# Reordering a written-out schedule: attention values one chunk earlier, turned norm tiles inside the feed-forward layer, ranking gathered before attention

## The reference

```
x = x + 0.5 * ffn(layernorm(x))
x = x + attn(layernorm(x))
x = x + 0.5 * ffn(layernorm(x))

ffn(x):   scores = x @ w_router; the 768 best of 1024 tokens: x <- gelu(x @ w_block); others keep x
attn(x):  Q = x @ Wq.T (16 heads of 32);  latent_k = x @ Wk_down.T;  latent_v = x @ Wv_down.T (64 wide)
          logits = (Q_h @ q_to_latent_h) @ latent_k.T / 8, causal; attn = softmax
          heads = (attn @ latent_v) @ v_up_h;  out = heads @ Wout.T
```

## Time and profile before

| | |
|---|---|
| median of 3 runs | 2322.88 us (2321.43 to 2325.64) |
| the profiled execution | 2322.91 us |
| its span | 2320.8 us |
| PE busy | 2143.9 us (92%) |
| DVE busy | 1762.1 us (76%) |
| ACT busy | 1099.7 us (47%) |
| POOL busy | 490.1 us (21%) |
| DMA, mean over 16 engines | 53 GB/s, 15% of their time |

### The profile page before, as it was taken

The page is one execution under the profiler, slowest core; times in us unless marked ns, Lnnn a source line. Parts: engine busy times, 40 slices in busy tenths (PEclk is TensorE's granted clock), DMA queues, the critical chain, the costliest instruction groups (busy, mean ns, idle before and its releaser), DMA issues.

```text
span 2320.8 us, 52537 instructions
## 1 busy us (share of the span) xinstructions
PE 2143.9 (92%) x21256; PEld 1305.3 (56%) x21256; DVE 1762.1 (76%) x5017; ACT 1099.7 (47%) x1942; POOL 490.1 (21%) x574
## 2 busy tenths in 40 slices
PE   5689999999999999999999999999999999999997
PEld 4444477545774456744566446764466544765446
DVE  6668857887678876798778886788857888578747
ACT  3335643556425554255543565445643456435562
POOL 3101212123112231023210232112221113121132
PEclk8789999999999999999999999999999999999999
DMA  4301021210312103021021211212021120212000
GB/s 140 145 1 37 4 73 48 99 39 2 99 48 74 38 18 94 38 74 39 20 91 38 75 39 36 74 56 67 29 69 41 66 83 2 73 37 74 2 2 37
DMA packets 71934, 123.16 MB, mean 53 GB/s; under 512 B 2832, under 2 KB 33040, under 8 KB 67600
## 3 DMA queue, kind: packets, MB, share of 16 engines
q1 hardware_dynamic: 71696, 119.81, 15.0%
HBM read 81.53 MB, written 37.75 MB: 51 GB/s over the span
## 4 chain that ended last, share of the span: by engine, by line
PE 77%; DVE 12%; ACT 5%; issue 4%; POOL 1%; DMA 1%; DVEq 0%; POOLq 0%; SPq 0%; ACTq 0%
PE psum L871 27%; PE psum L884 18%; PE psum L1011 11%; PE psum L1018 10%; PE psum L887 5%; DVE part L1160 3%; ACT pr L851 3%; PE psum L898 2%; DVE psum L1162 2%; PE psum L923 2%; DVE junk L1110 1%; DVE junk L1112 1%; PE psum L965 1%; DVE junk L1095 1%; DVE qk L1149 1%
## 5 line engine op out<-in xcount | busy, mean ns | idle before, releaser
L851 ACT ACTIVATE pr<-psum 128x512 f32<-128x512 f32 x1152 | 617.7, 597 | 528.9 <-PE psum L887 528.8
L884 PE MATMUL psum<-qk,qk 32*128 32x512 f32 (+3 forms) x4608 | 516.1, 370 | 62.6 <-DVE part L1160 26.7
L1162 DVE CUSTOM_DVE_ANT_0 psum<-psum,mask_b 128x512 f32<-128x512 f32 (+3 forms) x1024 | 473.1, 522 | 106.0 <-PE psum L898 104.0
L884 PEld LDWEIGHTS psum<-qk,qk 32*128 32x128 f32 x4608 | 318.6, 186 | 385.7 <-ACT pr L851 339.0
L898 PE MATMUL psum<-qk,qk 32*128 32x512 f32 (+3 forms) x4608 | 511.8, 370 | 21.5 <-DVE part L1160 18.8
L1160 DVE TENSOR_REDUCE part<-psum 128x1 f32<-128x512 f32 x512 | 325.1, 681 | 56.0 <-PE psum L898 53.7
L898 PEld LDWEIGHTS psum<-qk,qk 32*128 32x128 f32 x4608 | 311.2, 186 | 43.9 <-DVE part L1160 23.0
L1011 PE MATMUL psum<-pr,v_sb 128*32 128x512 f32 (+3 forms) x3072 | 314.1, 504 | 1.6 <-ACT ht L753 1.6
L1018 PE MATMUL psum<-pr,ones 128*32 128x512 f32 (+3 forms) x3072 | 306.8, 494 | 0.0
L745 POOL TENSOR_SCALAR_AFFINE_SELECT pr<-pr 128x512 f32<-128x512 f32 x256 | 161.6, 650 | 563.0 <-ACT pr L851 561.0
L871 PE MATMUL psum<-wb_h,nt_h 128*128 128x512 f32 x512 | 207.6, 405 | 16.2 <-DVE wb_l L1059 12.3
(11 more groups left out here) (116 smaller groups left out, 3372.8 us busy)
## 6 DMA issues: line engine op xcount, KB each, us to landing
nt_raw<-x_turned_dram SPq DMA_DIRECT2D x16, 1024.0 KB, 6.8
x<-x_dram SPq DMA_DIRECT2D x16, 1024.0 KB, 7.1
spill_x<-x SPq DMA_DIRECT2D x16, 1024.0 KB, 4.7
x<-spill_x SPq DMA_DIRECT2D x16, 1024.0 KB, 6.6
out_dram<-x SPq DMA_DIRECT2D x14, 1024.0 KB, 5.1
w_h<-scratch_o SPq DMA_DIRECT2D x28, 256.0 KB, 3.1
w_l<-scratch_o SPq DMA_DIRECT2D x28, 256.0 KB, 3.3
w_h<-scratch_q SPq DMA_DIRECT2D x6, 1024.0 KB, 4.9
```

Of the source, the lines that this page charges most:

```text
L851: nc.scalar.activation(pr_of(b, g, u)[:, 2 * p + place, :], bank(e, place), ACT.Exp, scale=SCALE).then_inc(exp_ready, 1)
L884: eng.matmul(o, (k_h, k_h, k_l)[t][own, P * j:P * (j + 1)], (q_h, q_l, q_h)[t][own, queries], start=(t == 0 and at == 0), stop=False, skip ...
L1162: m = nc.vector.tensor_tensor_reduce(scores, scores, mask_b[:, BANK - w:BANK], 1.0, FAR, ALU.add, ALU.max, top_of)
```

## The change

The values move from chunk 2n (unit n-2) to chunk 2n+1 (unit n-1), the denominators from chunk 2n+1 to chunk 2n; so the order PV(n-2), DEN(n-2) becomes DEN(n-2), PV(n-1), also at the end of group 3, where PV of unit 7 now stands in chunk 17. In `project` the first two turned tiles of the second norm go ahead of the last F. K and V of tiles 2 to 7 each stand a place or two earlier. In `back` NM goes behind the dots, both SC behind F of tile 2, and four of the eight RT stand before the attention instead of two. In `opening` the layer's F start after the ranking's events. Ring G gives way to an order of banks taken from `queue` at F of tile 2.

```diff
@@ opening
-        out += [("WC", 0), ("WS", 0)] + sum([raw(0, i) for i in range(TC, NT)], [])
+        out += [("WC", 0)] + sum([raw(0, i) for i in range(TC, NT)], [])
...
-        out += layer(0, 0, 0) + layer(0, 0, 1) + [("SC", 0, 0, 0), ("SC", 0, 0, 1), ("WS", 1), ("WS", 2)]
-        out += [("RT", 0, 0, i) for i in range(NT)]
-        for i in range(2, NT):
+        out += [("SC", 0, 0, 0), ("SC", 0, 0, 1), ("WS", 0)] + [("RT", 0, 0, i) for i in range(NT)] + [("WS", 1), ("WS", 2)]
+        for i in range(NT):
@@ project
-        out += layer(0, b, 6) + summed(b, 5) + [("NO", 1, b, 1)] + layer(0, b, 7)
-        after = [summed(b, 6), [], [], summed(b, 7) + scales(1, b, 1)]
-        for i in range(TC):
-            out += [("T", 1, b, i)] + ([("NO", 1, b, i + 2)] if i + 2 < TC else []) + left[i] + after[i]
+        out += [("NO", 1, b, 1)] + layer(0, b, 6) + [("T", 1, b, 0), ("NO", 1, b, 2), ("T", 1, b, 1), ("NO", 1, b, 3)]
+        out += summed(b, 5) + layer(0, b, 7) + left[0] + [("T", 1, b, 2)] + summed(b, 6) + left[1] + [("T", 1, b, 3)]
+        out += left[2] + left[3] + summed(b, 7) + scales(1, b, 1)
...
-        out += [("Q", b, 0, 1)] + loads[0] + keys[1] + [("V", b, 1)] + splits[0] + splits[1]
-        out += [("Q", b, 1, 1)] + loads[1] + maxima(b, 0, 0) + splits[2] + [("Q", b, 2, 1)] + loads[2] + maxima(b, 0, 1) + splits[3]
-        out += keys[2] + [("V", b, 2), ("Q", b, 3, 1)] + loads[3] + maxima(b, 0, 2) + keys[3] + [("V", b, 3)] + splits[4]
-        out += keys[4] + [("V", b, 4)] + splits[5] + maxima(b, 0, 3) + keys[5] + [("V", b, 5)] + splits[6]
-        out += keys[6] + [("V", b, 6)] + splits[7] + maxima(b, 0, 4) + keys[7] + [("V", b, 7)]
+        out += [("Q", b, 0, 1)] + loads[0] + pairs[1] + splits[0] + splits[1]
+        out += [("Q", b, 1, 1)] + loads[1] + maxima(b, 0, 0) + pairs[2] + splits[2]
+        out += [("Q", b, 2, 1)] + loads[2] + maxima(b, 0, 1) + pairs[3] + splits[3]
+        out += [("Q", b, 3, 1)] + loads[3] + maxima(b, 0, 2) + pairs[4] + splits[4] + pairs[5] + splits[5]
+        out += maxima(b, 0, 3) + pairs[6] + splits[6] + maxima(b, 0, 4) + pairs[7] + splits[7]
@@ attention
-            groups[g].append(combined(n, 0) + (then(n - 3, "HR") if n >= 3 else []) + (values(n - 2) if n >= 2 else []))
+            groups[g].append(combined(n, 0) + (then(n - 3, "HR") if n >= 3 else []) + (sums(n - 2) if n >= 2 else []))
             groups[g].append(combined(n, 1) + (then(n - 3, "HE") if n >= 3 else []) + mask(n) + [("MC", *e) for e in closes(n)]
-                             + ([("XT", *e) for e in closes(n - 1)] if n else []) + (sums(n - 2) if n >= 2 else []))
+                             + ([("XT", *e) for e in closes(n - 1)] if n else []) + (values(n - 1) if n >= 1 else []))
...
-        return groups, [then(last - 2, "HR") + then(last - 2, "HE") + values(last - 1), sums(last - 1), values(last),
+        return groups, [then(last - 2, "HR") + then(last - 2, "HE") + sums(last - 1), values(last), [],
@@ back
-        out += scales(2, b, 0) + added(4) + turn(3) + more(maxima, 6) + added(5) + turn(4) + dot(1, b, 0)
+        out += [("VA", 2, b, 0), ("RS", 2, b, 0)] + added(4) + turn(3) + more(maxima, 6) + added(5) + turn(4) + dot(1, b, 0)
...
-        out += scales(2, b, 1) + layer(1, b, 0) + turn(7) + more(turned, 0) + dot(1, b, 2) + dot(1, b, 3) + dot(1, b, 4)
-        out += layer(1, b, 1) + [("SC", 1, b, 0)] + dot(1, b, 5) + dot(1, b, 6)
-        out += layer(1, b, 2) + dot(1, b, 7) + layer(1, b, 3) + [("SC", 1, b, 1)]
-        out += layer(1, b, 4) + [("RT", 1, b, 0), ("RT", 1, b, 1)] + layer(1, b, 5)
+        out += [("VA", 2, b, 1), ("RS", 2, b, 1)] + layer(1, b, 0) + turn(7) + more(turned, 0) + dot(1, b, 2) + dot(1, b, 3)
+        out += dot(1, b, 4) + layer(1, b, 1) + dot(1, b, 5) + dot(1, b, 6) + dot(1, b, 7) + [("NM", 2, b, 0), ("NM", 2, b, 1)]
+        out += layer(1, b, 2) + [("SC", 1, b, 0), ("SC", 1, b, 1), ("RT", 1, b, 0)] + layer(1, b, 3) + [("RT", 1, b, 1)]
+        out += layer(1, b, 4) + [("RT", 1, b, 2)] + layer(1, b, 5) + [("RT", 1, b, 3)]
@@ group 0 of the next attention
-            groups[0][0] += [("F", 1, b - 1, 6), ("RT", 1, b - 1, 2), ("RT", 1, b - 1, 3)]
-            groups[0][1] += [("F", 1, b - 1, 7), ("G", 1, b - 1, 6), ("G", 1, b - 1, 7), ("RT", 1, b - 1, 4), ("RT", 1, b - 1, 5)]
+            groups[0][0] += [("F", 1, b - 1, 6), ("RT", 1, b - 1, 4)]
+            groups[0][1] += [("F", 1, b - 1, 7), ("G", 1, b - 1, 6), ("G", 1, b - 1, 7), ("RT", 1, b - 1, 5)]
@@ banks
+    behind, turns = list(range(6)), 0
+
     for e in sched:
...
+        if k == "F" and e[1] == 0 and e[3] == 2:
+            behind, turns = queue[1:5] + queue[:1] + queue[5:], 0
...
-            own = banks[e] = take("G", 0, 6, 1)
+            own = banks[e] = [behind[turns % 6]]
+            turns += 1
```

More of the change, by code:

```diff
@@ L176, in project @@
         loads = [[("W2", b - 1, "o", g)] for g in range(NQ)]
-        out += [("Q", b, 0, 1)] + loads[0] + keys[1] + [("V", b, 1)] + splits[0] + splits[1]
-        out += [("Q", b, 1, 1)] + loads[1] + maxima(b, 0, 0) + splits[2] + [("Q", b, 2, 1)] + loads[2] + maxima(b, 0, 1) + splits[3]
-        out += keys[2] + [("V", b, 2), ("Q", b, 3, 1)] + loads[3] + maxima(b, 0, 2) + keys[3] + [("V", b, 3)] + splits[4]
-        out += keys[4] + [("V", b, 4)] + splits[5] + maxima(b, 0, 3) + keys[5] + [("V", b, 5)] + splits[6]
-        out += keys[6] + [("V", b, 6)] + splits[7] + maxima(b, 0, 4) + keys[7] + [("V", b, 7)]
+        pairs = [keys[n] + [("V", b, n)] for n in range(NT)]
+        out += [("Q", b, 0, 1)] + loads[0] + pairs[1] + splits[0] + splits[1]
[3 more added lines that the diff above has]
+        out += maxima(b, 0, 3) + pairs[6] + splits[6] + maxima(b, 0, 4) + pairs[7] + splits[7]
         return out
```

## The result

| | before | after |
|---|---|---|
| median | 2321.43 us (2318.87 to 2325.64, 5 runs) | 2334.42 us (2333.54 to 2339.09, 5 runs) |
| ratio to before | | 1.0066, interval 1.0054 to 1.0078 |
| span of the profiled execution | 2320.8 us | 2331.8 us |
| mean granted clock of TensorE | 0.974 | 0.977 |

The account below looks back on a forecast made before the run. PE was taken to bound the kernel (77% of the chain), so order pays only where PE waits. Gains of 31.6 less losses of 22.8 took 2322.9 to 2314.1 us, range 2303 to 2325.

Parts of the forecast that it names:

- Group 3: End of group 3: PV of unit 7 waits 2.5 us for its mask on POOL in 7 batches; loss 17.6 us.
- Passages: Passage from group to group: the wait ahead of the next group goes, 0.1 lost ahead of unit 8; gain 13.9 us.
- the short cover only moves: Rival at the passages: the wait reappears ahead of unit 8 at 0.6 us, so slower, 2328.0 us; chance 0.14.
- Start of group 0: Attention's start: DVE reaches its reductions sooner and PV and DEN cover the waits; gain 10.5 us, plus 0.9 in batch 0.
- Banks of F: F of tile 2 in four batches: no more wait for a gelu behind a table load; gain 4.6 us.
- Opening: Start of the kernel: dots 4.2 us sooner, but wb_l made later and F ending later; loss 0.5 us.
- K and V: K, V and projections: the same reductions hold back the same MX, O starts 0.3 us later; loss 2.0 us.
- LAT's stretch: At LAT: T's low part ends later behind CB and ST of tile 6 on DVE; loss 2.7 us.
- In the last batch: Last batch: PV of unit 7 no longer waits 1.6 us for AC, the copy of unit 6's values; gain 1.7 us.
- SC and NM: SC's wait moves from first to second half, NM's DVE idle time goes to the wait for T 7; 0 us.
- Mask in time: Rival in group 3: RT and GX end 2.5 us sooner, the 17.6 are not paid; 2296.5 us, chance 0.07.
- start of group 0 stays bound: Rival: table load and woven CB take all but 1.4 of the 10.5; no difference, 2323.2 us, chance 0.25.

Follow-up runs that it names:

- the three sets of first scores above: First score's start in profiled executions: new order with queue 145.5 to 150.3 us (six), new order with ring's banks 140.2 to 140.6 (three), old order 142.4 to 144.4 (five).

## Why the prediction was wrong, point by point

Two steps failed: the loss in group 3 was priced too low, and most of the gain at the passages did not come. By the table above either alone would have left a sum near zero (the spans' +11.0 less 10.5 for the clock and what follows it in group 3 is +0.5; less 9.4 at the passages it is +1.6); together they made it a loss.

**Group 3.** The wait was found and its size was right: 2.74 us against 2.5. The step was priced at the idle time alone. The clock that halves behind it (1.3 us, six times), the 0.2 us between the idle time in brackets and what the wait costs from start to start, and F of tile 2 late behind the slowed F of tile 1 (2.7 in sum; it took 2.84 us in the one batch without the fall and 2.87 to 4.29 in the six with it) made it 31 instead of 17.6 (28.4 + 2.7). At 13 us this is the largest single error.

**Passages.** This is the step whose reasoning failed, by 9.4 us (by 11.0 if the passages themselves are taken alone). "I take a loss of 0.1" should have been 0.49: I followed the first reduction, but not which banks the pair of unit 8 gets once XT has taken one. By its own sign of being wrong, the exponentials' wait as before, this step had failed: it rose from 20.3 to 32.9. The rival "the short cover only moves" named 0.6 and the place; it happened, with 0.49, and I gave it 0.14. Its other half, the new wait deciding the sign, held too, but its sum of 2328.0 missed the clock.

**Start of group 0.** Right in its mechanism, and too small: 18.8 against 11.4. The order alone gave 11.8; the four RT ahead of the attention, which I had let end behind the same table load, gave 7.1 more. Of the order's 11.8, 3.2 are the clock: from unit 1 to unit 5 the batches behind the first took 19.83 to 20.86 us before, four of them over 20, and 19.83 with the new order. The changed kernel has 18.71 in seven of eight.

**Banks of F.** The gain of 4.6 came as 1.9, and as 4.7 once the wait of group 3 was out. What I did not see is that the same lines act in batch 0. I had put the opening's banks at nothing.

**Opening.** +0.5 was predicted (-1.4 if the column means kept their length, as they did), +2.1 measured in this pair and some +4.5 over all profiled executions: the order gains about 3, the banks lose about 7.5, as the means of the three sets of first scores above stand apart. The banks lose only with the new order: with the old one and the changed banks the first score starts at 143.4 us. The dots started 3.1 us sooner, not 4.2 (23.96 for 27.10). The row for the low part of the weights (w_l at 64.49 in the earlier trace rows) was moved by 5 us, to 69.44, not by the -0.2 to 1.3 I had, because F of tile 4 and the gelus behind it were late; with the queue from the second batch on it stands at 63.91.

**The others.** K and V (+2.2 for +2.0) and LAT's wait (0.89 for "about 0.9") are right. LAT's stretch came to +1.2 for +2.7: that the two T ahead of F of tile 7 "save nothing" was wrong, they save 4.4 under the new order. In the last batch the wait for AC went (1.65), but only 0.7 reached the end; what took the rest was not tried. SC and NM, taken at 0, cost 1.5, and the stretch from O to the second layer, which had no term, 1.7 by falls of the clock in other batches. "Mask in time" and "start of group 0 stays bound" did not happen.

## What to carry to other kernels

When a consumer is moved earlier, look in the *producer's* queue for work that stands ahead of its input only because nobody was in a hurry; here one line of order was worth 32 us. Price a wait of the matmul engine in the middle of dense work at its length and the slow clock that may follow: here 2.7 us of wait cost 4.2. And a rule that hands out banks by the state of a queue has to be followed bank by bank, at the odd event (here XT) and in the first round, where the state isn't yet what the rule assumes.

## What the runs showed of the hardware

- Behind a wait of 2.74 us TensorE's granted clock fell to 0.50 for 3.4 us in five of seven cases and for 6.8 us in a sixth; behind 1.2 us at the same place in one of seven. At the start of group 0 it fell in all seven batches of the kernel before, with waits of 1.79 and 1.83 us there. With the old ranking under the new order it fell in three of seven behind a wait of 1.78; behind one of 1.57 it fell in one of seven in the changed kernel, and in three of seven with the GX behind the mask. In the batch shown the clock had been full up to the wait. One fall cost 1.3 us where 3.4 us of dense PV and F lay behind it.
- The same periods also fell in the output projection, in different batches from run to run: the stretch from O to the second layer took 27.5 us without one and up to 29.2 with one. Executions of one kernel scatter by 2 to 3 us, and the clock goes with it: of the kernel before the fastest (2314.67 us) had a mean granted clock of 0.979, the slowest (2329.79) 0.969. That the falls make most of the scatter is my reading. So differences under 0.1% were read from stretches and not from medians.
